# Mamba stage of a macaron block on one Trainium2 core: three pairs of 512-column operations over two PSUM banks written as one operation of 1024 columns each

## What is computed

```python
x = x + 0.5 * ffn(layernorm(x))
x = x + mamba(n, weights1) + mamba(flip(n), weights2)      # n = layernorm(x)
x = x + 0.5 * ffn(layernorm(x))

def mamba(x, ...):                       # 256 inner channels, 16 states
    xi, z = split(x @ in_w.T)
    xc = silu(causal_conv(xi) + conv_b)
    dt, Bm, Cm = split(xc @ xp_w.T)
    delta = softplus(dt @ dtp_w.T + dtp_b)
    for t: h = h * exp(delta * A) + (delta * xc) * Bm ;  y = sum over states of h * Cm
    return ((y + xc * D) * silu(z)) @ out_w.T
```

## Time and profile before

| | us |
|---|---|
| three runs, median (lowest to highest) | 2793.95 (2793.76 to 2799.6) |
| profiled execution, its own time | 2819.37 |
| span from its first to its last instruction | 2817.6 |
| first mixture of experts and the way into Mamba | 0 to about 640 |
| Mamba, 32 units | about 640 to 2190 |
| second mixture of experts | about 2190 to the end |
| TensorE, VectorE, ScalarE, GpSimd busy in the span | 2293.6, 2255.0, 1901.1, 2198.0 |

### The profile page before, as it was taken

The page is one execution under the profiler, slowest core; times in us unless marked ns, Lnnn a source line. Parts: engine busy times, 40 slices in busy tenths (PEclk is TensorE's granted clock), DMA queues, the critical chain, the costliest instruction groups (busy, mean ns, idle before and its releaser), DMA issues.

```text
span 2817.6 us, 49017 instructions
## 1 busy us (share of the span) xinstructions
PE 2293.6 (81%) x15840; PEld 1958.7 (70%) x15840; DVE 2255.0 (80%) x3430; ACT 1901.1 (67%) x3628; POOL 2198.0 (78%) x1402
## 2 busy tenths in 40 slices
PE   5878888858898888888888989888887688888883
PEld 3778787736777767777667767677766477778773
DVE  8745555578999999999999999999999775555556
ACT  3344444438989999999999999999997334344441
POOL 3566666628999999999999999999999456666662
PEclk8999999989999999999999999999999789999996
DMA  7011111142333333333343333333333401111116
GB/s 231 19 40 38 40 40 39 39 148 84 106 106 101 108 102 110 105 107 104 106 105 108 103 110 103 103 111 102 108 107 102 150 16 41 40 38 39 39 40 192
DMA packets 155261, 248.60 MB, mean 88 GB/s; under 512 B 22066, under 2 KB 63954, under 8 KB 154322
## 3 DMA queue, kind: packets, MB, share of 16 engines
q1 hardware_dynamic: 136450, 202.92, 23.8%
q0 software_dynamic: 18208, 37.26, 4.9%
q10 hardware_dynamic: 432, 6.29, 0.6%
HBM read 213.10 MB, written 33.29 MB: 87 GB/s over the span
## 4 chain that ended last, share of the span: by engine, by line
PE 45%; issue 15%; DVE 15%; POOL 11%; ACT 9%; DMA 3%; another core or an unknown queue 1%; SPq 0%; ACTq 0%; POOLq 0%; DVEq 0%
PE bank L1337 14%; PE bank L1358 10%; POOL buf L542 8%; DVE buf L907 6%; PE bank L1533 6%; PE bank L1408 4%; PE bank L1508 3%; PE bank L1318 3%; ACT over L1150 2%; DMA buf<-state_rows 2%; ACT scaled L1183 2%; DVE buf L894 2%; POOL buf L529 2%; DVE bank L879 2%; DVE X L794 2%
## 5 line engine op out<-in xcount | busy, mean ns | idle before, releaser
L542 POOL TENSOR_TENSOR buf<-buf 128x1024 f32<-128x1024 f32 x512 | 1199.3, 2374 | 32.8 <-PE bank L1533 27.6
L907 DVE TENSOR_TENSOR_SCAN buf<-over,bank 128x512 f32<-128x512 f32 x832 | 954.0, 1201 | 4.5 <-PE bank L1508 2.4
L1337 PE MATMUL bank<-parts 128*128 128x256 f32 x3408 | 525.6, 300 | 82.7 <-issue 81.1
L1150 ACT ACTIVATE over<-wgu,negA 128x510 f32<-128x510 f32 x832 | 541.5, 709 | 40.1 <-DVE buf L907 28.8
L1337 PEld LDWEIGHTS bank<-parts 128*128 128x128 f32 x3408 | 457.1, 200 | 103.6 <-issue 99.1
L1533 PE MATMUL bank<-id_sb,buf 128*128 128x128 f32 x4096 | 517.6, 280 | 6.3 <-POOL buf L542 6.3
L491 POOL DMA_INDIRECT token_outputs<-buf,slot_out x284 | 295.3, 1040 | 289.4 <-ACT buf L1051 220.4
L1533 PEld LDWEIGHTS bank<-id_sb,buf 128*128 128x128 f32 x4096 | 479.9, 145 | 56.2 <-issue 46.8
L766 DVE TENSOR_TENSOR buf<-buf,bank 128x512 f32<-128x512 f32 x284 | 193.9, 684 | 333.4 <-ACT buf L1045 190.1
L1183 ACT ACTIVATE scaled<-wd_sb,I 128x256 f32<-128x256 f32 x896 | 377.3, 497 | 22.3 <-PE bank L1508 22.2
L481 POOL DMA_INDIRECT buf<-token_rows,slot_token x284 | 288.5, 1016 | 95.4 <-issue 88.9
(11 more groups left out here) (169 smaller groups left out, 2977.0 us busy)
## 6 DMA issues: line engine op xcount, KB each, us to landing
buf<-state_rows SPq DMA_DIRECT2D x608, 256.0 KB, 3.2
token_rows<-buf SPq DMA_DIRECT2D x32, 256.0 KB, 2.3
wd_sb<-token_outputs SPq DMA_DIRECT2D x16, 512.0 KB, 4.2
buf<-token_outputs SPq DMA_DIRECT2D x16, 512.0 KB, 5.2
buf<-token_rows,slot_token POOLq DMA_INDIRECT x284
token_outputs<-buf,slot_out POOLq DMA_INDIRECT x284
out<-X SPq DMA_DIRECT2D x16, 256.0 KB, 4.0
wgu<-wgT ACTq DMA_DIRECT2D x1, 2048.0 KB, 8.3
```

The costliest lines, as they stand in the source:

```text
L542: pool.tensor_tensor(hC[:, b, :].rearrange("p (c w) -> p c w", c=C), hs[:, b, :].rearrange("p (c w) -> p c w", c=C), Cs[:, b, :].unsqueeze ...
L907: V.tensor_tensor_scan(hs[:, b, w], dA[:, b, c, :, :].rearrange("p s t -> p (s t)"), source, 0.0, ALU.mult, ALU.add).then_inc(s[f"scan_don ...
L1150: ins = A.activation(dA[:, n % R, c, :, 1:], delta[r][:, c * W:(c + 1) * W].rearrange("p (s t) -> p s t", s=S)[:, :, 1:], ACT.Exp, scale=n ...
L1337: ins = M.matmul(bk[:, c * TP:(c + 1) * TP], w[:, b, cols], xx[:, b, :], start=(j == 0), stop=(j == 2))
```

## The change

The two absolute values become one operation on `pairs[3]`, which waits for the second half of the dt product. The two copies of the turned gated rows become one, which waits for both halves. The two gate products become one on `pairs[2]`; their wait was one already. The list `ACT_PRE` loses a name per direction, so that the counts stay right, and the copy raises its semaphore by 2.

```diff
 ACT_PRE = [f"{s}{r}" for r in (0, 1) for s in (
-    "xc0_", "xc1_", "z0_", "z1_", "hi", "abs0_", "abs1_", "exp", "ln")]
+    "xc0_", "xc1_", "z0_", "z1_", "hi", "abs", "exp", "ln")]
...
             def gate(u, r):
                 dve.wait_ge(s["y_done"], (u + 1) * NS)
                 wait(dve, s["pe_post"], 2 * u)
-                for h in range(S):
-                    ins = V.tensor_tensor(gat[:, h * W:(h + 1) * W], bank[4 + h], zs[r][:, h * W:(h + 1) * W], ALU.mult)
-                ins.then_inc(s["gated"], 1)
+                V.tensor_tensor(gat, pairs[2][:, :], zs[r], ALU.mult).then_inc(s["gated"], 1)
...
             def copy_gated(u):
 
-                for h in range(2):
-                    act.wait_ge(s["gT_pe"], 2 * u + h + 1)
-                    A.activation(gat[:, h * W:(h + 1) * W], bank[6 + h], ACT.Copy).then_inc(s["gT_done"], 1)
+                act.wait_ge(s["gT_pe"], 2 * u + 2)
+                A.activation(gat, pairs[3][:, :], ACT.Copy).then_inc(s["gT_done"], 2)
...
             def softplus_parts(p, r):
                 if r or p:
                     act.wait_ge(s["dve_pre"], done(DVE_PRE, f"delta{1 - r}", p - 1 + r))
-                for c, bk in ((0, bank[6]), (1, bank[7])):
-                    act.wait_ge(s["pe_pre"], done(PE_PRE, f"dt{c}_{r}", p))
-                    step(A.activation(tmp[:, c * W:(c + 1) * W], bk[:, :], ACT.Abs))
+                act.wait_ge(s["pe_pre"], done(PE_PRE, f"dt1_{r}", p))
+                step(A.activation(tmp, pairs[3][:, :], ACT.Abs))
 
             def log1pexp(p, r):
-                act.wait_ge(s["act_pre"], done(ACT_PRE, f"abs1_{r}", p))
+                act.wait_ge(s["act_pre"], done(ACT_PRE, f"abs{r}", p))
```

## The result

The changed kernel takes 2802.45 us in the median of its runs, the kernel before, measured beside it, 2793.76. Two of its 19 runs, 2891.15 and 3011.39 us with a mean granted clock of 0.82 and 0.74, are in a slower state; the ratio leaves them out, and the median of the other 17 is 2801.72. The ratio is 1.0027 with a 95% interval from 1.002 to 1.0033: some 7.5 us **slower**. The prediction said 2794.3 with a range up to 2799.0. It was wrong.

What follows compares the result with a forecast made beforehand. No engine full alone; a loop from GpSimd's buffer wait through VectorE, TensorE and ScalarE carries the time. Gates 0, absolute values 0, copies 0, end +0.34: 2793.95 + 0.3 = 2794.3 us, range 2790.5 to 2799.0.

Steps and rivals of the forecast that it cites:

- the gate's 0.07 us: VectorE's gate as one operation: done 0.07 us earlier, which ends at waits right behind it; taken as 0.
- ScalarE's slack at the residual: ScalarE's wait for TensorE at the residual, r = 0 unit: 0.57 us, to shrink to about 0.2 by absorbing the copy's delay.
- TensorE's wait at the spreading: TensorE's 0.42 us wait for a VectorE scan at the spreading of B, r = 0 units: to shrink to about 0.26.
- The loss at the very end: Last copy before the final `project_out`: +0.41 us, less the gate's 0.07, so +0.34 us.
- Worth nothing on the loop: Verdict on absolute values (0.16 us later) and copy (0.35 to 0.37 us later): later waits absorb both delays.
- 0 + 0: The sum's terms for absolute values and copies, each counted as costing no time.
- 0.83 us ahead of `project_out`: r = 0 unit: TensorE's `project_out` starts 0.83 us after the single copy's new end, so it is not delayed.
- Late absolute values hold TensorE where its granted clock is low: Rival: via logarithm to scaling, 0.16 us in some 9 slower-TensorE units, +1.4, giving 2795.7 us; chance 0.08.
- Two things wait for it: Behind the late copy: TensorE's `project_out`, and ScalarE's own next work, pushed back up to 0.37 us until the residual.
- The delays themselves: r = 0 unit, ScalarE: absolute values forecast to end 0.16 us later, the copy of turned rows 0.37 us later.
- The signs given for being wrong: GpSimd's waits moving more than a few us, or the residual no longer waiting while TensorE waits more for scalings.
- ScalarE's lateness gets through: Rival: ScalarE from step 8.5 to the residual late by 0.37 us a unit, 11.5 us over 31 units, 2805.8; chance 0.07.

## Why the prediction was wrong

**What was right.** The durations (gate 1.22, the others 1.02 to 1.03 where 1.01 was estimated); the gate's 0.07 us that ends in waits; ScalarE's slack at the residual nearly gone in the r = 0 unit; TensorE's wait at the spreading shrunk by the delay; 96.3 us for two units as before. The loss at the very end was forecast as 0.34 us. The last `project_out` starts 4.43 us after the last gate, at 2184.19, where it was 4.00 us before, 2194.36 less 2190.36; that is 0.43:

```profile
2188.62 1.22 PE L1456 MATMUL bank<-out_sb,buf 128*128 128x128 f32 x4 [1.17 <-ACT buf L1094]
```

Its wait was 0.69. In the steady state, then, the sum stands. The Trainium skill's rule (Perfetto Trace Analysis, Optimizing Scalar/DVE Operations) that breaking up the instructions of an engine that is not saturated, but holds others up, may let work be completed sooner is borne out by the copy and the absolute values: a single pair costs 0.3 us with the halves that start early, and 0.54 to 0.6 with the whole operations or with two halves that both start late.

**What failed.** The step that failed is "Worth nothing on the loop", said of the absolute values and of the copy and put into the sum as 0 + 0. The slack that it rested on was TensorE's 0.42 us at the spreading of B and 0.83 us ahead of `project_out` (in truth 0.4, at `turn_du`), and it exists in the steady units alone. Where the clock falls it is gone, and there each of the two costs 0.25 us a pair; and pairs with a low clock were more frequent and more often of the dear kinds.

1. *"Late absolute values hold TensorE where its granted clock is low"* was the right mechanism at the wrong price: 0.16 us in 9 units, +1.4, with a chance of 0.08. The absolute values alone cost some 4 us (1.0014), though 0.25 us in each of their five low pairs is only 1.2. I took the nine from a mean clock of 0.99 and read no unit in which it was low. The steady-state unit was taken for all. In the others the wait of 0.42 us, on which "worth nothing on the loop" rested, isn't there: TensorE's row at +30.32 shows no idle time.
2. *"Two things wait for it"*, of the copy, was incomplete. A third stands ahead of `project_out` in TensorE's order: `turn_du`, 12.5, which waits for the copy because it writes the bank that the copy reads. What was left there was not 0.83 us but some 0.4, and nothing in a unit with a low clock. This costs as much as the absolute values, 0.25 us a single pair.
3. The delays themselves were 0.25 and 0.49 us, not 0.16 and 0.37. I had the single operation start 0.03 us after the last matmul's row ends; it starts some 0.1 us after it, and the rows show ScalarE idle for 0.18 to 0.20 us ahead of it.
4. Not thought of at all: that the set of stretches changes. Single pairs rose from 0.3 to 0.9 us and double ones from 1.2 to 1.7 or 2.0. With the four pairs of the first profile of before at these prices that makes 2.4 of the 8.7 us of difference in excess, and with the five of the second 3.2 of 5.7 us. The rest, 6.3 and 2.5 us, is one early pair of 2.5 us in each profile of the changed kernel, and in the first two more double ones. An early pair stands also in the profile of the gate alone, where nothing starts late. Whether the change brings it, or chance, is not shown; it is in neither profile of before.

The signs given for being wrong did show: GpSimd's waits rose from 22.4 to 27.4 us, and TensorE waited 46.4 us for scalings instead of 36.2.

*"ScalarE's lateness gets through"*, 2805.8 with a chance of 0.07, gave a time nearer to the truth, by a mechanism that did not happen: not each unit is late by 0.37 us, but about one pair in two has a low clock, and those are late, by 0.9 to 2.5 us.

**What stays open.** Which pattern of work and idle time makes the clock fall, and why in one pair and not in another; and so, how much of the 7.5 us comes of the change itself and how much of where the stretches happened to lie. The gate alone came out at 1.0008, and on top of `turn_B` between the sums at 0.9998 where that alone had 0.9987. In both profiles an early pair stands, of 2.0 and 1.7 us, that their counterparts don't have; that the gate calls it is not shown.

## What to carry to other kernels

An operation that is made wider by merging halves starts when the last half is there; set the delay of the start against the few hundredths of a us that the merging saves, and list all that wait for the result in the order in which their engine comes to them, the writers of the buffer it reads among them. Read slack in the worst repetition, not in the steady one: windows of one repetition each show at once which are longer, and a mean clock of 0.99 can hide four pairs in fourteen. Where TensorE's clock falls now and then, it can pay to put work that others wait for ahead of work that nobody waits for yet; here one transposition moved ahead of one sum gained some 2.5 us, and moved ahead of its own operand it cost over 10.

## What the runs showed of the hardware

- The granted clock fell to half for 3.4 us at a time in a TensorE program that is busy for 84 of 96 us. How often changes with the order of its work: 11 stretches in Mamba in both profiles of the kernel before, 13 and 16 in the changed one, 21 to 32 where a transposition waits 0.64 us for its operand, some of them there 6.8 us long.
- The transfers are not what a stretch goes with: their share is 0.01 and 0.02 in the windows above, but also 0.03 at the same place of an undisturbed pair of before (1438.2 to 1441.2 us), and 0.52 in the second stretch of the changed kernel (1741.2 to 1744.2).
- What a stretch costs depends on where it falls and on what stands in the order around it: a single pair costs 0.02 us with `turn_B` between the sums, 0.3 before, 0.9 in the changed kernel, and an early pair 1.7 to 2.5.
- One operation over two PSUM banks instead of two over one: 1.224 against 1.29 us on VectorE, 1.03 against 1.05 to 1.07 on ScalarE.
- The expert stages around Mamba took 12.6 us longer each on some chips. The kernel before had its median at 2794 to 2795 us on some and at 2816 to 2819 on others, with the same Mamba.
